# Last attention of a hybrid two-layer model: a three-piece bias table, another order of SyncE's loads in short rounds, and weighing in bursts

## The reference

```python
q = (x @ Wq).reshape(b, n, HEADS, DIM_HEAD).transpose(0, 2, 1, 3) * scale
kv = x @ Wkv
k, v = (kv[..., :DIM_HEAD], kv[..., DIM_HEAD:])
sim = jnp.einsum('bhid,bjd->bhij', q, k)
...
sim = sim + jnp.transpose(bias, (2, 0, 1))[None] * bias_scale
sim = jnp.where(causal_mask[None, None], -neg, sim)
attn = jax.nn.softmax(sim, axis=-1)
out = jnp.einsum('bhij,bjd->bhid', attn, v)
out = out.transpose(0, 2, 1, 3).reshape(b, n, INNER)
return out @ Wout + bout
```

## Time and profile before

| what | before |
|---|---|
| runs, us | 3842.58, 3847.4, 3852.38 (median 3847.4) |
| the profiled execution, us | 3845.26 |
| its span, us | 3843.5 |
| mean granted TensorE clock, share of full | 0.898 |
| the stage: first lows to last, us from the span's start | 2650.9 to 3566.3 |
| busy in the whole span: PE / DVE / ACT / POOL | 83% / 62% / 48% / 24% |

### The profile page before, as it was taken

How to read it: one execution, slowest core, us unless ns; L and a number is a source line. 1 busy time by engine, 2 the same in 40 slices (tenths; PEclk the granted TensorE clock), 3 DMA queues, 4 the chain that set the end, 5 groups by cost and what they waited for, 6 DMA issues and landing times. The chain is left out here.

```text
span 3843.5 us, 68233 instructions
## 1 busy us (share of the span) xinstructions
PE 3181.4 (83%) x25621; PEld 1748.6 (45%) x25621; DVE 2368.5 (62%) x5084; ACT 1844.5 (48%) x3309; POOL 921.2 (24%) x732
## 2 busy tenths in 40 slices
PE   5748888885759999797699969998888888889899
PEld 2213333331337655573222227763555444555676
DVE  5457777772656455564599942236778777778322
ACT  3214555553226423363289925434555555555444
POOL 1007888894100223000000000001121112212100
PEclk8668999997879899896599969998999988999999
DMA  4112323221033000132422210028444335432100
GB/s 146 41 51 72 106 76 103 79 91 31 12 93 132 2 1 1 45 133 79 144 58 67 68 35 1 1 81 219 122 122 101 108 103 128 122 103 82 31 9 12
DMA packets 229588, 289.46 MB, mean 75 GB/s; under 512 B 44861, under 2 KB 164121, under 8 KB 226950
## 3 DMA queue, kind: packets, MB, share of 16 engines
q1 hardware_dynamic: 229303, 285.61, 25.0%
HBM read 229.49 MB, written 56.55 MB: 74 GB/s over the span
## 5 line engine op out<-in xcount | busy, mean ns | idle before, releaser
L1169 POOL TENSOR_TENSOR l0aa_e<-l0aa_e,l0aa_et 128x512 f32<-128x512 f32 x432 | 538.1, 1274 | 139.1 <-ACT l0aa_e L1311 139.1
L2407 ACT ACTIVATE l1ba_sg<-l1ba_sg,l1ba_mn 128x128 f32<-128x128 f32 (+7 forms) x512 | 394.1, 771 | 303.4 <-DVE l1ba_mn L2451 302.4
L2451 DVE CUSTOM_DVE_ANT_0 l1ba_sg<-l1ba_pS,l1ba_tab 128x128 f32<-128x128 f32 (+7 forms) x512 | 369.0, 745 | 167.4 <-PE l1ba_pS L2347 90.1
L2347 PE MATMUL l1ba_pS<-l1b_k,l1ba_qs 64*128 64x448 f32 (+7 forms) x2048 | 372.2, 470 | 103.5 <-DMA l1ba_qs<-l1b_qd 64.9
L1342 DVE TENSOR_REDUCE l0aa_low<-l0aa_pP 128x8 f32<-128x1024 f32 x288 | 342.2, 1220 | 164.4 <-PE l0aa_pP L1193 163.6
L2460 DVE STREAM_TRANSPOSE l1ba_pT<-l1ba_sg 128x1024 f32<-128x1024 f32 (+3 forms) x344 | 367.1, 1067 | 35.7 <-PE l1ba_pO L2367 32.3
L1311 ACT ACTIVATE l0aa_e<-l0aa_pS 128x512 f32<-128x512 f32 x432 | 257.0, 595 | 259.5 <-PE l0aa_pS L1226 152.7
L2367 PE MATMUL l1ba_pO<-l1ba_pT,l1ba_v 32*64 32x256 f32 x9216 | 324.0, 397 | 5.5 <-ACT l1ba_y L2422 4.6
L319 PEld LDWEIGHTS f_pY<-l_w,f_hT 128*128 128x128 f32 x2048 | 268.1, 192 | 123.8 <-issue 118.8
L2314 POOL TENSOR_TENSOR l1ba_co<-l1ba_co,l1ba_rb 128x1024 f32<-128x1024 f32 x64 | 151.1, 2360 | 709.6 <-ACT l1ba_co L2415 676.7
L2817 ACT ACTIVATE l1aa_e<-l1aa_e 128x1536 f32<-128x1536 f32 x192 | 284.6, 1484 | 43.2 <-DVE l1aa_e L2858 25.9
(11 more groups left out here) (398 smaller groups left out, 5008.1 us busy)
## 6 DMA issues: line engine op xcount, KB each, us to landing
f_wB<-l0f_weights SPq DMA_DIRECT2D x16, 2048.0 KB, 7.2
l1ba_qs<-l1b_qd SPq DMA_DIRECT2D x128, 256.0 KB
l1ba_tab<-l1b_table SPq DMA_DIRECT2D x64, 512.0 KB
l1ba_rb<-l1b_rdd SPq DMA_DIRECT2D x64, 512.0 KB
l0aa_et<-l0a_table SPq DMA_DIRECT2D x16, 1536.0 KB
l1b_qd<-l1bp_part SPq DMA_DIRECT2D x64, 256.0 KB, 2.3
l0aa_et<-l0a_table SPq DMA_DIRECT2D x16, 512.0 KB
l0aa_qs<-l0a_qd SPq DMA_DIRECT2D x64, 96.0 KB
```

The costliest lines, as they stand in the source:

```text
L1169: nc.gpsimd.tensor_tensor(es, es, t, ALU.mult).then_inc(multiplied, 1)
L2347: ins = nc.tensor.matmul(pS[n % 2][:, at:at + half], qs[lo:lo + HALF, r % 2, i + k, :], ks[lo:lo + HALF, key:key + half], start=True, stop ...
L2407: nc.scalar.activation(row, row, ACT.Exp, bias=mn[:, r % 2, i + k:i + k + 1], scale=-1.0, accum_out=den[:, r % 2, i + k:i + k + 1]).then_i ...
L2451: nc.vector.tensor_tensor_reduce(row, scores, bias, 1.0, 3e38, ALU.add, ALU.min, mn[:, r % 2, h:h + 1]).then_inc(m_done, 1)
```

## The change

Three edits in `attention_strips`:

1. The near half of the table is split: columns 0 to 255 keep the semaphore `near_in`, columns 256 to 511 get `mid_in`. The mid pieces (4 DMAs of 256 KB) are loaded as soon as B2's lows are made, the last that use them; the near pieces (4 of 256 KB) as before behind B0's. VectorE's lows wait for the mid piece too where the width is over 256.
2. SyncE's `spread_sums(r - 1)` comes behind the loads in B1 too, as it did in B0 alone: queries of B7' and then the reciprocals of B2.
3. A weighing that ran in `units - 1` shares behind successive units runs in `units // 2` bursts behind every second unit. In B6 to B4 this is 4 bursts for 7 shares (the 16 pairs of B7 as 4, 4, 4, 4 for 2, 2, 2, 3, 2, 2, 3), in rounds with 4 units 2 for 3; with 2 units or 1 it stays one.

```diff
-        near_in, far_in = ([sem(f"{n}{i}") for i in range(HG // 2)] for n in ("near_in", "far_in"))
+        near_in, mid_in, far_in = ([sem(f"{n}{i}") for i in range(HG // 2)] for n in ("near_in", "mid_in", "far_in"))
...
             for i in range(HG // 2):
-                load_table(0, i, 0, GROUP, near_in)
+                load_table(0, i, 0, 2 * P, near_in)
+                load_table(0, i, 2 * P, GROUP, mid_in)
                 load_table(0, i, GROUP, SEQ, far_in)
...
             for r in range(ROUNDS):
-                if r and block_of(r):
+                u = block_of(r)
+                if r and u > 1:
                     spread_sums(r - 1)
                 if r + 2 < ROUNDS:
                     load_queries(r + 2)
-                if r + U < ROUNDS and block_of(r) in (GROUP_BLOCKS, 0):
+
+                piece = {4: (GROUP, SEQ, far_in), 2: (2 * P, GROUP, mid_in), 0: (0, 2 * P, near_in)}.get(u)
+                if piece and r + U < ROUNDS:
                     sp.wait_ge(m_done, (r + 1) * HG)
                     for i in range(HG // 2):
-                        if block_of(r):
-                            load_table(r // U + 1, i, GROUP, SEQ, far_in)
-                        else:
-                            load_table(r // U + 1, i, 0, GROUP, near_in)
-                if block_of(r) == 0:
+                        load_table(r // U + 1, i, *piece)
+                if u <= 1:
                     spread_sums(r - 1)
...
                 for r in range(ROUNDS):
                     first, units = FIRST[r + 1] + 2, FIRST[r + 2] - FIRST[r + 1]
-                    if units > 1:
-                        first, units = first + 1, units - 1
-                    if first <= n < first + units:
-                        weigh(r, (n - first) * pairs(r) // units, (n - first + 1) * pairs(r) // units)
+                    bursts = max(units // 2, 1)
+                    k = (n - first) // 2
+                    if 0 <= k < bursts and n - first - 2 * k == (units > 1):
+                        weigh(r, k * pairs(r) // bursts, (k + 1) * pairs(r) // bursts)
...
                     dve.wait_ge(near_in[h // 2], 16 * (G + 1))
+                    if width(r) > 2 * P:
+                        dve.wait_ge(mid_in[h // 2], 16 * (G + 1))
                     if width(r) > GROUP:
                         dve.wait_ge(far_in[h // 2], 16 * (G + 1))
```

## The result

The change makes the kernel slower: 3890.7 us median (3875.9 to 3892.9) against 3846.4, a ratio of 1.011 with a 95% interval of 1.0083 to 1.0138. 3812 was forecast, with 3850 as the upper end.

A forecast was written before the change was run, and what follows sets the result against it. VectorE was taken as the bound, interrupted by waits for table, scores and weighing. Tables and queue order -36 us, start +1, bursts 0: -35 from 3847.4 gives 3812 us, range 3772 to 3850.

The forecast's parts named there:

- its catch: Change of group, SyncE queue: B2's reciprocals stand behind mid and queries, so their broadcast is 2.5 us later.
- signs of being wrong: VectorE's score waits over 120 us in total, or a group change still taking 29 us from broadcast to second turn.
- R + 5.9 + 3.3 + 2.3, plus 1.4 to be seen: Queries of B7' usable at R + 12.9 instead of R + 17.6; R is the issue of B3's reciprocals' broadcast.
- the 7.7 us from the broadcast to the first lows: Change of group: transfers 1.5 + 2.3 + 0.8 plus 3.1 fixed, from B2's broadcast to VectorE's first lows.
- part 1: Tables in three pieces with queries ahead, at seven changes of group: 5.1 us gained at each, 36 us in all.
- B7' second scores 1, project 2, weighing of B1 1.99 put its end near R + 23.5 at worst: TensorE at a group change: B1's weighing ends before VectorE needs it at R + 25.1, so both turn waits go.
- the sum: Change of group: second turn's distance 29.8 - 25.1 = 4.7 us, with 0.4 of a stall 5.1, counted seven times: 36 us.
- part 2: Weighing in bursts, 11 calls fewer a group: forecast zero, between 23 us of gain and 34 us of loss.
- I take zero, because the two periods of rows 7 are equal.: Quiet B6 units: VectorE's period 2.01 us, TensorE's 2.00 with two pairs, so bursts gain nothing.
- rival (c): VectorE idles behind bursts, 0.85 us per stalled unit; with 10 stalled a group 33 us slower, 3880; chance 0.1.
- Rival (b): Each spared weighing call counts because TensorE holds most units: -36 - 23 + 1, 3789 us; chance 0.15.

The follow-up runs named there:

- early copies: Kernel before with only the queue's new order in B1, plus ScalarE copying B2's result and B3's projection ahead of B7' first unit's exponentials: 0.9928 of before.
- the order alone: Kernel before with only the queue's new order in B1 (queries of B7' ahead of B2's reciprocals), table in two pieces: 0.9988 of before.
- with the tables: The change without its bursts, plus ScalarE taking B2's result and B3's projection ahead of the exponentials of B7' first unit: 0.9990 of before.
- the bursts alone: Kernel before with only the new loop around weigh; tables, queries and reciprocals as before: 1.0058 of before.
- tables and order alone: The change with the old weighing shares: tables in three pieces and the queue's new order, against the kernel before: 1.0037.
- doubled scores: Scores of each third unit in B7 to B3 made twice: with the weighing bursts 1.0015 of before; in the kernel before 0.9983.

## Why the prediction was wrong

**Right:** what the queue does, and its catch. The mid pieces hold the reciprocals of B2 back and so the near table. The queries of B7' go out at R + 4.9, and TensorE waits 1.6 us for them for 6.5 (means of seven). B4 gained 0.2, and B1 gave back 0.8 of the 0.9 that B2 lost. Two of the prediction's own signs of being wrong came true: over 120 us of waits for scores (130.2), and a second turn 29 us or more behind R (32.0).

**Mis-sized:** the step "R + 5.9 + 3.3 + 2.3, plus 1.4 to be seen", and the 7.7 us from the broadcast to the first lows. Mid and queries of B7' were usable at R + 14.1 on the mean, not R + 12.9. At the change shown the queue moved less than the 315 and 230 GB/s that I took and ended in a slow tail, so their data were over near R + 14.6, not R + 11.5. The broadcast was at R + 14.2 on the mean and not R + 13.3. From it to the first lows took 8.7 us for 7.7; that the change shown has 7.65 (2881.90 to 2889.55) is luck, it is the shortest of the seven. First lows stood at R + 22.9 instead of R + 21.0. Earlier than before by 0.4 in the forecast, they were later by 1.0.

**Wrong, part 1 (forecast -36 us, measured +14):** the step "B7' second scores 1, project 2, weighing of B1 1.99 put its end near R + 23.5 at worst". It followed TensorE alone. Between the two weighings stand a copy and a projection, and the copy is in ScalarE's queue behind an exponential that waits for the very table whose wait was to be filled. The second turn stood at R + 32.0 on the mean, not R + 25.1. The early copies take this out: with the order alone B7 went from 25.1 to 21.0 and the turn to R + 24.0. Nor does an earlier turn count in full, as the sum had it: that kernel's turn is 5.8 us earlier than before at seven changes, 41 us, and its stage 30 us shorter; with the tables it is 3.3 us earlier, 23 us, and the stage is as long as before.

**Wrong, part 2 (forecast 0, measured +22):** "I take zero, because the two periods of rows 7 are equal." The periods were right and VectorE is the bound in quiet units. But here the time spared on TensorE, which isn't the bound, became idle time ahead of a projection that waits for ScalarE, and the granted clock falls: 19 slow projections for 7 with the bursts alone, about 1.6 us each, in front of scores that VectorE waits for. (Of the 27 of the whole change, seven are B3's at the changes of group; they are slow with tables and order alone too and belong to part 1.) I had read the slow weighing in the earlier trace rows as a cost of idling and didn't ask where the bursts would put their idle time. That is about 12 of the bursts' 26 us in the stage. The other 14 are mostly what rival (c) describes, VectorE idle behind the first burst that follows a late projection, 0.8 us in B3 and in B2, two blocks that I had worked out as even. So (c), at a chance of 0.1, had the sign and about half of the cause. Rival (b) is refuted: every spared call did not count, it cost.

The Trainium skill ("TensorE: Matmul & The Clock Gate", Part 1) names idle gaps as what brings the clock down to 1.2 GHz; the trace of the bursts alone agrees in kind, with a projection of 3.54 us, for 2.02, behind a gap of 2.05.

## What to carry to other kernels

Before moving a load or a step ahead, follow its consumers through every engine's program order, not only the one that was seen waiting: the next thing in some queue may wait for exactly what the move was to cover. Where TensorE isn't the bound, fewer or denser instructions on it may be no gain, and were a loss here, where the idle time gathered ahead of a step on the path; look at the granted clock of that step. And of two loads behind one another, send first the one that is waited for.

## What the runs showed that was not expected

Repeating matmuls made kernels faster: about 0.7 us of doubled scores in each round from B7 to B3 took 17 us off the bursts' kernel and 13 off the one with order and early copies. In the kernel before they took off 5 us of the stage and nothing clear of noise in the runs. The engine was hardly less busy ahead of the projection in the slow case (14.89 of 16.0 us, then a gap of 2.05) than in the fast one (15.29 of 15.8, then 1.40), and the projection took 1.5 us more.
